# A sorting kernel: each row as two interleaved lanes of 512 places, merged by the last level

## The chip, the core and the metric

The kernel runs on one core of a Trainium2 chip. The core has five engines that run their own instruction streams and meet at semaphores: PE (TensorE, matrix products into the PSUM banks), DVE (VectorE, elementwise work on 128 partitions), ACT (ScalarE, activations), POOL (GpSimd, here only for gathers by index) and SP (SyncE, here only for transfers). The metric is the device time of one execution in microseconds (us). Smaller is better.

## What is computed

Eight images of 32 x 32 places with 128 channels pass through a deformable convolution, a self-correlation with a sort, a windowed attention, a mixture of experts, a state space model and a second mixture of experts. The part that matters here is the second one. Each image has 1024 tokens. For every token the correlation with all 1024 tokens is sorted in descending order and 128 fixed ranks of it are kept:

```python
def _L1_conv_ref(x):
    x3 = x.reshape(b, m, c)                      # m = 1024 tokens, c = 128
    corr = jnp.einsum('bmc,bnc->bmn', x3, x3) / c
    x_sort = jnp.sort(corr, axis=-1)[..., ::-1]
    ranks = jnp.round(jnp.linspace(1.0, m - 1, NB_POOLS)).astype(jnp.int32)
    return x_sort[..., ranks]
...
x = x + _L0_conv_ref(_gn(x), ...)
x = x + _L1_conv_ref(_gn(x))
t = t + _L2_attn_ref(...); t = t + _L2_ffn_ref(...)
t = t + _L3_attn_ref(...); t = t + _L3_ffn_ref(...)
```

## The kernel before

**Units.** The sort works in units of half an image: 4 tiles of 128 tokens, so that a buffer of a unit (`corr`, `srt_a`, `srt_b`) holds 4 x 1024 values in each of 128 partitions. There are 16 units, two for each image (h = 0 and h = 1), and the whole sort is done by DVE (`dve_S`).

**Streams.** Besides the sort (letter S) there are three streams. F is the front of the next image: group norm, the deformable convolution with its 24 groups of gathers (POOL gathers, PE and ACT combine), the second group norm, and the correlation (`pe_corr`, `act_corr`). C is attention, first experts and state space model of a half image that is already sorted. M is the second mixture of experts. Each engine runs one instruction stream, in which a table of letters (`ORDER`, one string for each engine and stage) says from which stream the next step is taken (`weave`). Nothing is reordered at run time: an instruction that waits holds up all that stands behind it on its engine. The stages are fill (F of image 0), early (sort of image 0 beside F of image 1), full (a body for each of the images 1 to 6, five of them in a loop), late (image 7) and drain.

**The first exchange is made by the correlation.** `sd` holds sums and differences of pairs of token columns. PE forms products with the sums and with the differences, ACT takes the absolute value of the latter, and PE adds and subtracts it, so that ACT writes to `corr` the larger and the smaller of each pair (L695, 512 values at a time). Before the change a pair is two columns 128 apart, and each write goes to runs of 128.

**The start of a unit.** `corr` is seen as 8 blocks of 128 places. The rest of a sorting network for 8 inputs runs across these blocks (L808 to L834 and again L808/L810), so that each of its operations reads and writes runs of 128. Its outputs have to become sorted groups of 8 neighbours, so the last results go to the view `Y`, with a step of 8 values (32 bytes) from one value to the next:

```python
X, L, R, Y = places(corr), places(srt_a), places(srt_b), corr[:].rearrange("p g (r s) -> p g s r", s=8)
```

`corr` is also used for this, so it is only given back to ACT (`corr_used`) once the first merge operation of runs of 16 (L796) has read it.

**The merges.** For run lengths m = 16 to 512 sorted runs are merged: a comparison of the two halves (`compare`, L794 the larger, L796 the smaller), then steps of distance k = m/4 down to 1 (L873 and L881 in one direction, L893 for the step m/8 in place, L901 and L903 back), with small copies of the edges (L877, L880) in the steps that change the buffer. Then the whole row of 1024 is merged by a comparison with the second half read backward (`hi[:, :, ::-1]`) and halvings down to 16, and only the places of the wanted ranks go through the last three steps (L927). L936 adds the ranks to the image; from there the stream C of this half starts.

**Links.** Dependent operations of one stream on DVE are tied by a semaphore (`link.put`, `link.wait`). `dve_gn` (L537, L540) takes the statistics of a group norm for F. L1073 on DVE needs the square root that ACT writes at L1063.

Of the kernel before, what the change touches and what calls it, by code (L numbers as in the profile page):

```python
# [62 lines left out]
        "FFFFFFFFFFFFFFCFFFFCCFFCFFCCCFFFFFCCFFFCCFCCFCCFFCCFFFFFFFFFFFFCCCCCCCCCCCCCCCCCCCCCCCCCCCCCCCCC"  # L63
# [3 lines left out]
        "FFFFFFFFFFFFFFFFFFFFFFFFFFFFFFFFFFFFFFFFFFFFFFFFFFFFCFCCFCFFFCCCFCCCFFFCCFFFFFFFFFFFFCCCCCCCCCCC"  # L67
# [42 lines left out]
    DVE_late=(  # L110
        "MCSSCMSSSSSSSSSSCCMSSCCMSSMSSSMSSCMSSCMSSSSSCSSCMCSSCMCSSCMSSSSSMSSSSMSSSSMSSSSSSSMSSCMSSCMSSSSM"
        "SSSSSCSSCSSCMSSCMCSSCCMSSCMSSCMCSSSSSCMSSMSSCCMSSSSCCMSSMSSCCMSSCMSSCMSSCMMSSMSSSSMSSMSMSMSMSMCS"
        "SCSSMSSSSMSSCCMSSCCMSSMSSCSSSCMSSSSCMCSSCMCSSSCMCSSSSMSSSSMSSSSSMSSSSSSCMSSCMSSSMSSSSSSCSSCMSSCM"
        "SSCMCSSSCCSSCMSSCMCMSSCSSMSSCCMSSMSSCSSSCSSCCSSSSCSSCSSCSSSSSSSSSSSSSSSSSSSS"
    ),
    DVE_drain=(
        "MCMCMMMMMMCCCMCMCMCMMCCCCCCMMMCMCCCMCMCCCCMCMCCMCMCCMMCCMCCMCCMCMMMMMMMMMMMMMMMMMMMMMMMMMMMMMMMM"
# [3 lines left out]
        "MCMCCCMMMMCMMCCCCCMMMMMMMCCMMMMMCCCCCMCCCMCCCMCCCCCCCCCCCMCCMMMCMMMCMCCCCCCCCMCMCMMMMMMMCMMCMMMC"  # L121
        "MMMMMCCMMMMMMCCMMMMCCMMMCMCMMMCMMMMMMMMMMMMMMMMMMMMMMMMMMMMMMMMMMMMMMMMMMMMMMMMMMMMMMMMMMMMMMMMM"
# [3 lines left out]
        "MCMCCMCMCCCMMCMCMMCMCCCMCMCMMCCMMCCCCCMCCCCCCCCCCCMMCMCCMCCCMCCCCCCCCCCCMMCMMCCMMMCMCMCMCMMCCMCM"  # L126
        "CCMCCMMCCMMMMMMMMMMMMMMMMMMMMMMMMMMMMMMMMMMMMMMMMMMMMMMMMMMM"
# [19 lines left out]
def build(nc, A, IMGS=IMAGES):  # L147
# [3 lines left out]
    with ctx:  # L151
# [65 lines left out]
        sd = sb("sd", [P, 2, 4, P])  # L217
# [395 lines left out]
        def pe_corr(pe, i, h):  # L613
# [4 lines left out]
            for t in range(4 * h, 4 * h + 4):  # L618
# [3 lines left out]
                sums, diffs = (sd[:, k].rearrange("p s r -> p (s r)") for k in range(2))  # L622
# [62 lines left out]
        def act_corr(act, i, h):  # L685
            for t in range(4 * h, 4 * h + 4):
# [1197 lines left out]
```

## Time and profile before

| | us |
|---|---|
| median of 3 executions | 4932.3 (4931.25 to 4941.95) |
| profiled execution | 4926.9 |
| its span | 4925.1 |
| DVE busy in the span | 4278.7 (87%) |
| PE busy in the span | 3975.1 (81%) |
| ACT busy in the span | 2954.3 (60%) |
| POOL busy in the span | 894.7 (18%) |

The span is the time from the first to the last instruction in the trace. Engines work beside each other, so busy times don't add up. Average shares hide the stages: DVE has nothing to sort before 248.65 us (fill) and after 4601 us (drain), and is busy nearly all of the time between. DVE starts its next instruction before the one before has quite ended: from start to start two independent operations lie some 0.08 us less apart than the duration of the first.

### The profile page before, as it was taken

How to read it: one execution, taken by the hardware profiler on the slowest of the kernel's cores; microseconds unless marked ns; L12 is line 12 of the kernel's file. 1: busy time of each engine (PE TensorE's matmuls, PEld its weight loads, DVE VectorE, ACT ScalarE, POOL GpSimd, SP SyncE). 2: the span in 40 equal slices, each digit the busy share in tenths (PEclk: the TensorE clock that was granted, in tenths of full speed). 3: DMA queues.
4: the chain of work that ended last, by engine and by line, in shares of the span. 5: the costliest groups of instructions: out<-in, count | busy, mean ns of one | idle time of the engine just before them, and what ended most of it. 6: DMA issues, size and time to landing. Idle time of an engine off the chain costs nothing.

```text
span 4925.1 us, 59870 instructions
## 1 busy us (share of the span) xinstructions
PE 3975.1 (81%) x19410; PEld 2674.8 (54%) x19410; DVE 4278.7 (87%) x5380; ACT 2954.3 (60%) x7241; POOL 894.7 (18%) x580
## 2 busy tenths in 40 slices
PE   5747748989798988989798988989798987767587
PEld 3616424667456654567456654566456653545354
DVE  1098999999999999999999999999999999999521
ACT  4526526687467846687467846687467855555452
POOL 2317000242005300242005300242005210000000
PEclk8878869999899988999799988999799988978798
DMA  4314100232013210232013210232013210010001
GB/s 131 98 35 124 35 0 18 75 101 69 5 43 110 79 36 18 75 102 68 7 43 110 79 36 18 67 104 67 13 43 109 71 40 13 22 29 27 10 22 39
DMA packets 226079, 269.71 MB, mean 55 GB/s; under 512 B 26831, under 2 KB 188506, under 8 KB 225626
## 3 DMA queue, kind: packets, MB, share of 16 engines
q0 software_dynamic: 46080, 151.03, 10.6%
q1 hardware_dynamic: 179674, 114.65, 7.9%
q8 instruction: 167, 2.74, 0.2%
q14 instruction: 158, 1.29, 0.1%
HBM read 242.25 MB, written 23.34 MB: 54 GB/s over the span
## 4 chain that ended last, share of the span: by engine, by line
PE 38%; DVE 33%; issue 12%; ACT 9%; DMA 4%; POOL 3%; SPq 1%; DVEq 0%; another core or an unknown queue 0%; ACTq 0%; POOLq 0%
PE bank L597 6%; PE bank L1633 4%; PE bank L1628 4%; PE bank L1613 3%; PE bank L1298 3%; POOL gath L759 3%; DMA gath<-quads,idx 3%; DVE srt_b L873 2%; DVE srt_b L881 2%; DVE srt_a L796 2%; DVE srt_b L796 2%; PE bank L569 2%; PE bank L1225 2%; PE bank L1218 2%; DVE srt_a L893 2%
## 5 line engine op out<-in xcount | busy, mean ns | idle before, releaser
L759 POOL DMA_INDIRECT gath<-quads,idx x576 | 894.5, 1553 | 3083.4 <-DVE idx L722 2005.3
L597 PE MATMUL bank<-diag,gath 128*128 128x128 f32 x4608 | 612.4, 295 | 167.6 <-DMA gath<-quads,idx 166.8
L639 ACT ACTIVATE diag<-ident,w 128x128 f32<-128x128 f32 x2304 | 704.6, 393 | 20.3 <-DVE w L737 20.2
L597 PEld LDWEIGHTS bank<-diag,gath 128*128 128x128 f32 x4608 | 591.3, 210 | 203.1 <-DMA gath<-quads,idx 126.9
L1613 PEld LDWEIGHTS bank<-e2w,act 128*128 128x128 f32 (+1 forms) x3072 | 409.8, 198 | 161.7 <-issue 157.3
L1628 PE MATMUL bank<-mu_t,e2w 128*128 128x512 f32 (+1 forms) x768 | 424.0, 635 | 86.4 <-DMA e2w<-moe_w_t 39.9
L1633 PE MATMUL bank<-gated_u,e2w 128*128 128x512 f32 (+1 forms) x768 | 426.1, 638 | 34.2 <-DVE act L1713 31.9
L1713 DVE TENSOR_TENSOR act<-act,bank 128x512 f32<-128x512 f32 (+1 forms) x384 | 261.3, 680 | 180.0 <-PE bank L1633 159.5
L1613 PE MATMUL bank<-e2w,act 128*128 128x128 f32 (+1 forms) x3072 | 415.0, 282 | 1.6 <-DVE act L1713 1.6
L873 DVE TENSOR_TENSOR srt_b<-srt_a 128x1024 f32<-128x1024 f32 x192 | 351.3, 1830 | 1.2
L881 DVE TENSOR_TENSOR srt_b<-srt_a 128x1024 f32<-128x1024 f32 x192 | 351.0, 1828 | 0.0
L1681 ACT ACTIVATE act<-bank 128x512 f32<-128x512 f32 (+1 forms) x384 | 227.7, 593 | 201.5 <-PE bank L1628 198.8
L1681 ACT ACT_TABLE_LOAD x199 | 255.3, 1283 | 11.9 <-PE bank L1628 8.8
L672 ACT ACTIVATE cols<-bank 128x384 f32<-128x384 f32 x192 | 93.0, 484 | 245.1 <-PE bank L597 235.7
L1633 PEld LDWEIGHTS bank<-gated_u,e2w 128*128 128x128 f32 (+1 forms) x768 | 131.3, 188 | 186.7 <-issue 140.0
L794 DVE TENSOR_TENSOR srt_b<-srt_a 128x2048 f32<-128x2048 f32 x96 | 219.6, 2287 | 1.4
L794 DVE TENSOR_TENSOR srt_a<-srt_b 128x2048 f32<-128x2048 f32 x96 | 219.5, 2286 | 0.9
L796 DVE TENSOR_TENSOR srt_a<-srt_b 128x2048 f32<-128x2048 f32 x96 | 219.2, 2284 | 0.0
L796 DVE TENSOR_TENSOR srt_b<-srt_a 128x2048 f32<-128x2048 f32 x96 | 219.2, 2283 | 0.0
L901 DVE TENSOR_TENSOR srt_a<-srt_b 128x2016 f32<-128x2016 f32 (+1 forms) x96 | 211.8, 2206 | 0.9
L903 DVE TENSOR_TENSOR srt_a<-srt_b 128x2016 f32<-128x2016 f32 (+1 forms) x96 | 211.7, 2205 | 0.0
L1628 PEld LDWEIGHTS bank<-mu_t,e2w 128*128 128x128 f32 (+1 forms) x768 | 122.1, 188 | 148.3 <-issue 62.1
(348 smaller groups left out, 8161.5 us busy)
## 6 DMA issues: line engine op xcount, KB each, us to landing
e2w<-moe_w_t SPq DMA_DIRECT2D x256, 170.5 KB
quads<-xn_tok SPq DMA_DIRECT2D x256, 64.0 KB
e1w<-L_ffn_w SPq DMA_DIRECT2D x256, 64.0 KB, 1.9
e2w<-moe_w_t SPq DMA_DIRECT2D x256, 64.0 KB
gath<-quads,idx POOLq DMA_INDIRECT x576
e2w<-moe_w_t SPq DMA_DIRECT2D x128, 42.5 KB
x_tok<-x SPq DMA_DIRECT2D x8, 512.0 KB, 4.1
out<-tm SPq DMA_DIRECT2D x16, 256.0 KB, 2.3
```

Of the source, the lines that this page charges most:

```text
L597: ins = T.matmul(FB[q % 2][:, k * P:(k + 1) * P], gath[:, g % 2, k, s * C:(s + 1) * C], diag[:, g % 2, 4 * k + s], start=(s == 0), stop=(s ...
L639: ins = SC.activation(diag[:, g % 2, n], ident[:], ACT.Copy, scale=w[:, n:n + 1])
L759: pool.indirect_dma_start(gath[:, g % 2, k], None, quads, bass.IndirectOffsetOnAxis(idx[:, TG * g + k:TG * g + k + 1], 0)).then_inc(sem["g ...
L794: V.tensor_tensor(dst[:, :, 0:size // 2], lo, hi, ALU.max)
L796: return V.tensor_tensor(dst[:, :, size // 2:size], lo, hi, ALU.min)
L873: V.tensor_tensor(out_lo, lo, hi, ALU.max)
L881: link.put(V.tensor_tensor(out_hi, lo, hi, ALU.min))
L1613: ins = T.matmul(MB[2][:, t * P:(t + 1) * P], act2[0:m, n % ACT2_SLOTS, t * P:(t + 1) * P], e2w[0:m, e % 2, W2 + k * C:W2 + (k + 1) * C], ...
L1628: T.matmul(MB[r % 2][0:m, :], e2w[:, e % 2, k * P:k * P + m], mu_t[:], start=True, stop=True).then_inc(sem["m_ps"], 1)
L1633: T.matmul(MB[r % 2][0:m, :], e2w[:, e % 2, W3 + k * P:W3 + k * P + m], gated_u[:], start=True, stop=True).then_inc(sem["m_ps"], 1)
L1681: SC.activation(act2[0:m, n % ACT2_SLOTS], MB[r % 2][0:m, :], ACT.Silu).then_inc(sem["m_sb"], 1)
L1713: V.tensor_tensor(act2[0:m, n % ACT2_SLOTS], act2[0:m, n % ACT2_SLOTS], MB[r % 2][0:m, :], ALU.mult).then_inc(sem["hh"], 1)
```

## The change

The row is held as two lanes of 512 places that are neighbours in memory: lane 0 at the even, lane 1 at the odd addresses. The pairs that the correlation exchanges are now the columns j and j + 512, and ACT writes the larger of two such columns and the smaller of them alternately, two values at a time at a step of 4. So each lane has sorted runs of two from the start. The network across 8 blocks is gone. The merges by halves start at m = 8 memory places (runs of four in each of two lanes) and go on to m = 1024, with steps down to k = 2, which is distance 1 within a lane. The runs of four have a short form of their own, with one operation in place and one copy. Then the two lanes are merged by one comparison, lane 0 forward against lane 1 backward, which also puts the lanes apart; the halvings go on from 512 as before. The strings of letters for the engines in the stages early, full, late and drain are new as well (two of the many lines are shown).

```diff
     PE_early=(
-        "FFFFFFFFFFFFFFFFFFFFFFFFFFFFFFFFFFFFFFFFFFFFFFFFFFFFFCFCCFCFFFCCCFCCCFFFCCFFFFFFFFFFFFCCCCCCCCCCC"
+        "FFFFFFFFFFFFFFFFFFFFFFFFFFFFFFFFFFFFFFFFFFFFFFFFFFFFFFFFFFFFCCCFCCCCCCCFFFFCCFFFFFFFFCCCCCCCCCCC"
...
-        sd = sb("sd", [P, 2, 4, P])
+        sd = sb("sd", [P, 2, HALF])
...
-                there = corr[:, t % UT].rearrange("p (s k r) -> p s k r", k=2, r=P)
+                there = corr[:, t % UT].rearrange("p (b k w) -> p b k w", k=2, w=2)
...
-                    SC.activation(there[:, :, k], FB[1 - k][:].rearrange("p (s r) -> p s r", r=P), ACT.Identity,
+                    SC.activation(there[:, :, k], FB[1 - k][:].rearrange("p (b w) -> p b w", w=2), ACT.Identity,
                                   scale=0.5 / C).then_inc(sem["corr_sb"], 1)
...
-            V.tensor_tensor(sd[:, 1], pairs[:, :, 0], pairs[:, :, 1], ALU.subtract)
-            V.tensor_tensor(sd[:, 0], pairs[:, :, 0], pairs[:, :, 1], ALU.add).then_inc(sem["sd"], 1)
+            V.tensor_tensor(sd[:, 1], yn_t[:, 0:HALF], yn_t[:, HALF:TOK], ALU.subtract)
+            V.tensor_tensor(sd[:, 0], yn_t[:, 0:HALF], yn_t[:, HALF:TOK], ALU.add).then_inc(sem["sd"], 1)
...
-            X, L, R, Y = places(corr), places(srt_a), places(srt_b), corr[:].rearrange("p g (r s) -> p g s r", s=8)
...
-            yield from exchange(fours(X, 0), fours(X, 1), fours(R, 0), fours(R, 1))
...
-            V.tensor_tensor(Y[:, :, 0], R[:, :, 0], R[:, :, 4], ALU.max)
-            link.put(V.tensor_tensor(Y[:, :, 7], R[:, :, 3], R[:, :, 7], ALU.min))
...
-            yield from exchange(L[:, :, 2:4], L[:, :, 4:6], R[:, :, 2:4], R[:, :, 4:6])
-            yield from exchange(R[:, :, 1:7:2], R[:, :, 2:7:2], Y[:, :, 1:7:2], Y[:, :, 2:7:2])
-            now = 1
-            m = 16
-            while m < TOK:
...
+            ins = yield from compare(8, runs(corr, 8), runs(srt_a, 8))
+            ins.then_inc(sem["corr_used"], 1)
+            yield
+            dve.wait_ge(sem["corr_used"], unit("corr_used", i, h))
+            now = 0
+            m = 8
+            while m <= TOK:
...
                 k = m // 4
-                while k >= 1:
+                while k >= 2:
                     lo, hi = pairs(here, k)
                     out_lo, out_hi = pairs(there, k)
                     link.wait()
                     V.tensor_tensor(out_lo, lo, hi, ALU.max)
                     yield
-                    if k == 1:
-
-                        V.tensor_copy(edges(there, 0, 1), edges(here, 0, 1))
+                    if m == 8:
+
+                        link.put(V.tensor_tensor(hi, lo, hi, ALU.min))
+                        yield
+                        link.wait()
+                        link.put(V.tensor_copy(lo, out_lo))
+                        yield
+                        break
+                    if k == 2:
+
+                        V.tensor_copy(edges(there, 0, 2), edges(here, 0, 2))
...
-            k = TOK
+            pair = bufs[now][:].rearrange("p g (j w) -> p g j w", w=2)
+            lo, hi = pair[:, :, :, 0], pair[:, :, ::-1, 1]
+            half = bufs[1 - now][:].rearrange("p g (w j) -> p g w j", w=2)
+            link.wait()
+            V.tensor_tensor(half[:, :, 0], lo, hi, ALU.max)
+            yield
+            link.put(V.tensor_tensor(half[:, :, 1], lo, hi, ALU.min))
+            yield
+            now = 1 - now
+            k = TOK // 2
```

What this makes of DVE's stream in one unit: 158 instructions become 157. 146 comparisons of two operands become 144, and the values that they write come to 184,304 in each partition, before and after. 12 copies (2,160 values) become 13 (3,184).

**Place 1: DVE, the first unit.** A row gives line, operation, output and inputs, and the shape of the output with its dimensions. Before, the end of the network across blocks and the first merge operations; the first and the third pair of rows write to `Y`:

```order
L833 TENSOR_TENSOR corr<-srt_b 128x512
L834 TENSOR_TENSOR corr<-srt_b 128x512
L808 TENSOR_TENSOR srt_b<-srt_a 128x4x256
L810 TENSOR_TENSOR srt_b<-srt_a 128x4x256
L808 TENSOR_TENSOR corr<-srt_b 128x4x3x128
L810 TENSOR_TENSOR corr<-srt_b 128x4x3x128
L794 TENSOR_TENSOR srt_a<-corr 128x256x8
L796 TENSOR_TENSOR srt_a<-corr 128x256x8
```

After, the unit's first rows, where nothing stands ahead of them:

```order
L791 TENSOR_TENSOR srt_a<-corr 128x512x4
L793 TENSOR_TENSOR srt_a<-corr 128x512x4
L830 TENSOR_TENSOR srt_b<-srt_a 128x512x2
L834 TENSOR_TENSOR srt_a<-srt_a 128x512x2
L837 COPY srt_a<-srt_b 128x512x2
L791 TENSOR_TENSOR srt_b<-srt_a 128x256x8
L793 TENSOR_TENSOR srt_b<-srt_a 128x256x8
L830 TENSOR_TENSOR srt_a<-srt_b 128x256x4
```

The rows of 128x512 and 128x4x3x128 into `corr` are gone, and the last reader of `corr` (L793) is the unit's second instruction, where it was its eighteenth (L796).

**Place 2: DVE, the end of the merges in the same unit.** Before, the last step of m = 512, the comparison of the whole row (L794 and L796 of 128x4x512, their second input read backward), the next halving:

```order
L901 TENSOR_TENSOR srt_a<-srt_b 128x8x255
L903 TENSOR_TENSOR srt_a<-srt_b 128x8x255
L794 TENSOR_TENSOR srt_b<-srt_a 128x4x512
L796 TENSOR_TENSOR srt_b<-srt_a 128x4x512
L794 TENSOR_TENSOR srt_a<-srt_b 128x8x256
L796 TENSOR_TENSOR srt_a<-srt_b 128x8x256
```

After, the last step of m = 1024, the comparison of the lanes (L877, L879), the next halving:

```order
L866 TENSOR_TENSOR srt_a<-srt_b 128x4x255x2
L868 TENSOR_TENSOR srt_a<-srt_b 128x4x255x2
L877 TENSOR_TENSOR srt_b<-srt_a 128x4x512
L879 TENSOR_TENSOR srt_b<-srt_a 128x4x512
L791 TENSOR_TENSOR srt_a<-srt_b 128x8x256
L793 TENSOR_TENSOR srt_a<-srt_b 128x8x256
```

The comparison of the whole row is replaced by one of the same size that reads every second value.

**Place 3: the stage early, behind the first unit.** DVE before; `lnsd` at L1073 is written by ACT (the square root of C's first norm):

```order
L936 TENSOR_TENSOR tc<-x2_tok,srt_a 128x512
L959 BN_STATS lnst<-tc 128x6 x4
L967 BN_AGGR lnmv<-lnst 128x2 x4
L808 TENSOR_TENSOR srt_b<-corr 128x8x256
L810 TENSOR_TENSOR srt_b<-corr 128x8x256
L1073 RECIPROCAL lnsd<-lnsd 128x4
L1074 SCALAR_TENSOR_TENSOR nmr<-lnmv,lnsd 128x4
L818 TENSOR_TENSOR corr<-srt_b 128x8x128
L820 TENSOR_TENSOR corr<-srt_b 128x8x128
```

DVE after, where L1047 is the former L1073:

```order
L910 TENSOR_TENSOR tc<-x2_tok,srt_a 128x512
L933 BN_STATS lnst<-tc 128x6 x4
L941 BN_AGGR lnmv<-lnst 128x2 x4
L791 TENSOR_TENSOR srt_a<-corr 128x512x4
L793 TENSOR_TENSOR srt_a<-corr 128x512x4
L1047 RECIPROCAL lnsd<-lnsd 128x4
L1048 SCALAR_TENSOR_TENSOR nmr<-lnmv,lnsd 128x4
L537 BN_STATS bst<-yn_t 128x6
L540 BN_STATS bst<-yn_t 128x6
L542 BN_AGGR mv<-bst 128x2
```

ACT before, where L672 and L639 are F's groups of gathers (a copy out of PSUM and twelve diagonal matrices for the group after next):

```order
L672 ACTIVATE cols<-bank0 128x384
L639 ACTIVATE diag<-ident,w4 128x128 x12
L1063 ACT_TABLE_LOAD
L1063 ACTIVATE lnsd<-lnmv,eps_ln 128x4
L672 ACTIVATE cols<-bank1 128x384
L639 ACTIVATE diag<-ident,w4 128x128 x12
L973 ACTIVATE tbu<-tc,nmr,lnsd 128x128 x4
L1079 ACTIVATE arena<-ident 128x4x96
L672 ACTIVATE cols<-bank0 128x384
```

ACT after, where L1037 is the former L1063:

```order
L672 ACTIVATE cols<-bank0 128x384
L639 ACTIVATE diag<-ident,w4 128x128 x12
L672 ACTIVATE cols<-bank1 128x384
L672 ACTIVATE cols<-bank0 128x384
L1037 ACT_TABLE_LOAD
L1037 ACTIVATE lnsd<-lnmv,eps_ln 128x4
L681 ACTIVATE xn_tok<-bank1 128x128
L521 ACTIVATE yn_t<-bank0 128x512
L521 ACTIVATE yn_t<-bank1 128x512
L947 ACTIVATE tbu<-tc,nmr,lnsd 128x128 x4
```

On ACT the square root stood behind 19 of image 1's 24 groups and now stands behind all 24; on DVE the statistics L537 and L540 of F now stand right behind its reciprocal, and stood behind 31 more rows, most of them of the sort.

## Rows read from the trace of the kernel before

**Rows 1.** The page's first part: busy us, share of the span, instructions.

```profile
PE 3975.1 (81%) x19410; PEld 2674.8 (54%) x19410; DVE 4278.7 (87%) x5380; ACT 2954.3 (60%) x7241; POOL 894.7 (18%) x580
```

**Rows 2.** Busy time by stretch: early, one full body, late, drain (header gives columns).

```profile
core 0: us, PE busy (x) PEld busy (x) DVE busy (x) ACT busy (x) POOL busy (x), PEclk, DMA share, GB/s
248.65:735.61 486.96, 283.25 (x1305) 195.65 (x1306) 466.09 (x477) 197.70 (x551) 113.28 (x72) 0.77 0.17 49
1842.10:2398.15 556.05, 484.76 (x2426) 328.10 (x2426) 533.41 (x672) 369.65 (x908) 118.92 (x72) 0.92 0.20 59
4067.29:4601.01 533.72, 366.49 (x1554) 228.53 (x1554) 520.56 (x624) 260.37 (x556) 0.00 (x0) 0.83 0.07 21
4601.01:4925.10 324.09, 262.08 (x1126) 167.21 (x1126) 77.91 (x214) 162.23 (x346) 0.00 (x0) 0.87 0.09 27
```

**Rows 3.** Groups of DVE instructions by shape: operation, count, busy us, mean ns, idle.

```profile
L794 DVE TENSOR_TENSOR srt_a<-srt_b 128x2048 f32<-128x2048 f32 x96 | 219.5, 2286 | 0.9
...
L808 DVE TENSOR_TENSOR corr<-srt_b 128x1536 f32<-128x1536 f32 x16 | 47.0, 2938 | 0.1
...
L833 DVE TENSOR_TENSOR corr<-srt_b 128x512 f32<-128x512 f32 x16 | 17.4, 1090 | 0.0
...
L927 DVE TENSOR_TENSOR srt_a<-srt_b 128x84 f32<-128x84 f32 x64 | 16.8, 304 | 0.0
...
L822 DVE TENSOR_TENSOR srt_a<-srt_b 128x512 f32<-128x512 f32 x16 | 10.9, 682 | 0.0
...
L877 DVE COPY srt_b<-srt_a 128x512 f32<-128x512 f32 x16 | 10.3, 642 | 0.0
...
L927 DVE TENSOR_TENSOR srt_b<-srt_a 128x336 f32<-128x336 f32 x16 | 8.0, 501 | 0.0
```

**Rows 4.** DVE in order of time, the unit's start: start us, us, operation.

```profile
1853.03 1.08 DVE L833 TENSOR_TENSOR corr<-srt_b 128x512 f32<-128x512 f32 x1
1853.95 1.10 DVE L834 TENSOR_TENSOR corr<-srt_b 128x512 f32<-128x512 f32 x1
...
1862.76 2.92 DVE L808 TENSOR_TENSOR corr<-srt_b 128x1536 f32<-128x1536 f32 x1
1865.53 2.92 DVE L810 TENSOR_TENSOR corr<-srt_b 128x1536 f32<-128x1536 f32 x1
```

**Rows 5.** DVE in order of time, in the merges (copies, dependent and independent neighbours).

```profile
1929.35 0.29 DVE L880 COPY srt_a<-srt_b 128x256 f32<-128x256 f32 x1
...
1931.60 2.16 DVE L901 TENSOR_TENSOR srt_b<-srt_a 128x1920 f32<-128x1920 f32 x1
1933.68 2.15 DVE L903 TENSOR_TENSOR srt_b<-srt_a 128x1920 f32<-128x1920 f32 x1
1935.86 2.23 DVE L873 TENSOR_TENSOR srt_a<-srt_b 128x1984 f32<-128x1984 f32 x1
...
3020.29 0.41 DVE L880 COPY srt_b<-srt_a 128x256 f32<-128x256 f32 x1
```

**Rows 6.** L794's instructions by form: duration ns min/median/max, first and last start.

```profile
L794 DVE TENSOR_TENSOR srt_b<-srt_a x96: 2259/2291/2294, 305.4 to 4590.3; 128x2048 f32<-128x2048 f32 x96
```

**Rows 7.** ACT's group of writes to `corr`, by shape.

```profile
L695 ACT ACTIVATE corr<-bank 128x512 f32<-128x512 f32 x128 | 74.6, 595 | 130.8 <-PE bank L627 54.3 <-PE bank L630 50.7 <-DVE srt_a L796 25.7
```

**Rows 8.** ACT in order of time, stage early: start us, us, operation, idle before.

```profile
273.80 1.08 ACT L695 ACTIVATE corr<-bank 128x512 f32<-128x512 f32 x2 [23.37 <-DVE srt_a L796]
...
294.49 1.08 ACT L521 ACTIVATE yn_t<-bank 128x512 f32<-128x512 f32 x2 [0.81 <-PE bank L510]
...
362.20 0.49 ACT L672 ACTIVATE cols<-bank 128x384 f32<-128x384 f32 x1 [3.56 <-PE bank L597]
...
481.33 0.49 ACT L672 ACTIVATE cols<-bank 128x384 f32<-128x384 f32 x1 [3.64 <-PE bank L597]
...
486.64 0.30 ACT L1063 ACTIVATE lnsd<-lnmv,eps_ln 128x4 f32<-128x4 f32 x1
```

**Rows 9.** DVE in order of time, stage early, behind the first unit.

```profile
471.49 2.28 DVE L810 TENSOR_TENSOR srt_b<-corr 128x2048 f32<-128x2048 f32 x1
486.97 0.18 DVE L1073 RECIPROCAL lnsd<-lnsd 128x4 f32<-128x4 f32 x1 [13.20 <-ACT lnsd L1063]
```

More of the change, by code:

```diff
@@ L94 @@
-        "CMSSCMSSMSSSSSSSCSSCMSSCMSSCMCSSCCMSSCMSSSCMCSSSSCSSCCSSSSCCFFSSCCFSSSSCFSSCFSSCSSSSSSSSSS"
+        "MCSSCMSSSSSMSSMCCMSSSCCMSSMSSMCSSSCSSMSSCMCSSCMCFCFCMFSSSMSSMSSSSSSSSSSSSSCMSSCMFSSMSSSSSSSSSCCS"
+        "SCMSSCMCSSCCMSSSSSCSSCSSCMFSSFSSCMFFSSCCMFSSCCMSSMSSSCSSCMSSSSCMSSCMSSCMSSSSMSSMSSMMSSMSSSSMSSMS"
+        "MSMSMSMCSSCSSSSSMSSSSSCCMSSCCMSSSSSSSSSCMSSCSSSMSSMCSSCSSCSSCMCSSSCMSSMSSSSMSSSSMSSSSSMSSSSSSMSS"
+        "CMSSCMSSSSSSSSSCSSCMSSCMSSCMCSSCCFFCMFSSSCMCMFSSCFSSMSSCSSCMSSCMCSSSSCCSSCSSCSSCSSSSSSSSSS"
@@ L621, in pe_corr @@
                 mine = yn_t[:, t * P:(t + 1) * P]
-                sums, diffs = (sd[:, k].rearrange("p s r -> p (s r)") for k in range(2))
+                sums, diffs = sd[:, 0], sd[:, 1]
                 T.matmul(FB[0][:], mine, diffs, start=True, stop=True).then_inc(sem["corr_mm"], 1)
@@ L742, in dve_pre @@
             dve.wait_ge(sem["corr_sb"], img("corr_sb", i, 0))
-            pairs = yn_t[:].rearrange("p (s k r) -> p s k r", k=2, r=P)
-            V.tensor_tensor(sd[:, 1], pairs[:, :, 0], pairs[:, :, 1], ALU.subtract)
-            V.tensor_tensor(sd[:, 0], pairs[:, :, 0], pairs[:, :, 1], ALU.add).then_inc(sem["sd"], 1)
+            V.tensor_tensor(sd[:, 1], yn_t[:, 0:HALF], yn_t[:, HALF:TOK], ALU.subtract)
+            V.tensor_tensor(sd[:, 0], yn_t[:, 0:HALF], yn_t[:, HALF:TOK], ALU.add).then_inc(sem["sd"], 1)
             yield
@@ L814, in fours @@
-            def fours(buf, b):
-                return buf.rearrange("p g (a b c) r -> p g a b (c r)", a=2, b=2)[:, :, :, b]
-            yield from exchange(fours(X, 0), fours(X, 1), fours(R, 0), fours(R, 1))
-            V.tensor_tensor(X[:, :, 1::4], R[:, :, 1::4], R[:, :, 2::4], ALU.max)
-            yield
-            link.put(V.tensor_tensor(X[:, :, 2::4], R[:, :, 1::4], R[:, :, 2::4], ALU.min))
-            yield
-            V.tensor_tensor(L[:, :, 3], R[:, :, 3], R[:, :, 7], ALU.max)
-            link.wait()
@@ L834, in dve_S @@
-            link.put(V.tensor_tensor(Y[:, :, 7], R[:, :, 3], R[:, :, 7], ALU.min))
-            yield
-            link.wait()
-            yield from exchange(L[:, :, 2:4], L[:, :, 4:6], R[:, :, 2:4], R[:, :, 4:6])
-            yield from exchange(R[:, :, 1:7:2], R[:, :, 2:7:2], Y[:, :, 1:7:2], Y[:, :, 2:7:2])
-            now = 1
-            m = 16
-            while m < TOK:
-                first = m == 16
-                if not first:
+            ins = yield from compare(8, runs(corr, 8), runs(srt_a, 8))
@@ L844, in dve_S @@
+            ins.then_inc(sem["corr_used"], 1)
+            yield
+            dve.wait_ge(sem["corr_used"], unit("corr_used", i, h))
+            now = 0
+            m = 8
+            while m <= TOK:
+                if m > 8:
                     link.wait()
-                ins = yield from compare(m, runs(corr if first else bufs[now], m), runs(bufs[1 - now], m))
-                if first:
-                    ins.then_inc(sem["corr_used"], 1)
-                else:
+                    ins = yield from compare(m, runs(bufs[now], m), runs(bufs[1 - now], m))
@@ L849, in dve_S @@
                     link.put(ins)
-                yield
-                if first:
-                    dve.wait_ge(sem["corr_used"], unit("corr_used", i, h))
-                now = 1 - now
+                    yield
+                    now = 1 - now
                 here, there = runs(bufs[now], m), runs(bufs[1 - now], m)
@@ L906, in dve_S @@
                 m *= 2
-            k = TOK
+            pair = bufs[now][:].rearrange("p g (j w) -> p g j w", w=2)
[6 more added lines that the diff above has]
+            yield
+            now = 1 - now
+            k = TOK // 2
             while k >= 16:
```

85 lines of the change are left out of this document (31 added, 54 removed).

## The prediction

> **What bounds the kernel now.** I read the busy times first: DVE is busy 87% of the span, PE 81% [rows 1]. The stretches say more. In a full body, of which there are six, DVE is busy 533.4 of 556.05 us and idle 22.6; PE is busy 484.8 of them at a granted clock of 0.92, and ACT 369.7. In late DVE is busy 520.6 of 533.7, in early 466.1 of 487.0, and only in drain does it have little to do [rows 2]. So from the first unit of the sort to the last, 248.65 to 4601 us, the time is DVE's own work plus 23 us of gaps for each image. What leaves DVE's stream there shortens the time nearly one for one, unless PE, which has 71 us of air in a full body, can't follow. Fill and drain lie on chains in which nothing of the sort changes.
>
> **What a comparison costs.** 2048 values take 2286 ns (L794) and 512 values 682 ns (L822) [rows 3]. That is (2286 - 682) / (2048 - 512) = 1.044 ns a value and 147 ns for the instruction. Neighbours that don't depend on each other start 2.08 us apart at a duration of 2.16 [rows 5], so on the path an instruction costs its duration less 0.08. Where the next one depends on it the distance is 2.18, 0.10 more [rows 5].
>
> **The slow writes go.** By this rule 1536 values cost 1.75 us, but the two writes of 1536 into `Y` take 2.94; and 512 values cost 0.68, but L833 takes 1.09 [rows 3]. These four operations (L808, L810, L833, L834) are the ones that write single values 32 bytes apart. From start to start they show 2.77 and 0.92 us [rows 4], where 1.67 and 0.60 would be due. Gone with them are 2 x 1.10 + 2 x 0.32 = 2.84 us in a unit. The number of compared values stays at 184,304, so the rest of the network across blocks is not saved: it comes back as merges of runs of four and as the level m = 1024. Two instructions fewer give 2 x 0.07 = 0.14.
>
> **What the new patterns cost.** Three forms are new. Runs of two values at a step of 32 bytes (L830, L834 at m = 8): L927 with 336 values (42 cells of 8, two of each) reads and writes just this form in 501 ns, and 147 + 336 x 1.044 is 498, so there is no surcharge; L927 with 84 values, which it reads singly 32 bytes apart, needs 304 where 235 would be due [rows 3]. Every second value, forward and backward (L877, L879): before, the whole-row comparison reads its second input backward by single values, and L794's longest of 96 took 2294 ns, 3 above the median [rows 6]; steps of two forward are in the last steps k = 1 of each merge. The two together are in no row. Upper bound: L833's rate, (1090 - 147) / 512 = 1.84 ns a value or 3.92 us for 2048, 1.55 us more on the path for each of the two, 3.1 in a unit; lower bound 0. I take 0, because these addresses lie 8 bytes apart and not 32. A gain I exclude: no comparison in the trace beats 1.04 ns. ACT's writes of two values at a step of four: 595 ns now [rows 7]; bounded above by the same surcharge of 0.41 us, 0 below. The 128 writes would cost 52 us of ACT, spread over a span in which ACT has 186 us of air in each full body [rows 2]; only the eight before the first unit would lie on the path, 3.3 us. I take 0.
>
> So the trace tells single values at 32 bytes (slow) from pairs at 32 bytes (not slow) [rows 3]. The Trainium skill gives a reason (Advanced Engine Details and Errata, SBUF Cachelines): lines of 16 bytes, and at least two hits on a line are needed for full rate. By that rule all three new forms have two hits and cost nothing extra, as I take it, and L833's form has one.
>
> **Copies.** The unit gets a copy of 1024 values in runs of two (L837). A copy of 256 takes 0.29 us where the values come in runs and 0.41 where they stand alone [rows 5]; 512 single ones take 0.64 [rows 3]. So 1024 in runs cost 0.15 + 4 x 0.14 = 0.71 us, 0.63 on the path, and at the rate of single ones 1.05. I take 0.63, as they come in runs. The other copies turn from single values into pairs, and those of the first merge (512 single ones) drop out: in sum 0.45 less. Net +0.2.
>
> **Links.** At m = 8 the operation in place, the copy and the next comparison each wait for the one before; two bare links at 0.10 us are 0.2, and about half as many go elsewhere. +0.1.
>
> **Sum for a unit:** -2.84 - 0.14 + 0.2 + 0.1 = -2.7 us. With 12 units in the full bodies and 2 in late this is -38 us, if PE and ACT follow. Why they should: `corr` is free again after the unit's second instruction, no longer after its eighteenth, so that the second half's correlation and with it F can start some 20 us earlier (30 in the full body), and the new tables have moved F forward on all engines. There PE and ACT get air just where the first 100 us of a body held them up.
>
> **The stage early** has the same -5.4 us for its two units, but a wait that grows. Before, ACT found `corr` free at 273.8 us [rows 8] (23 us of waiting for L796). After, the second comparison ends 4.4 us behind 248.65, at 253.1: F starts 20.7 us earlier, and its first copy of gathered columns (L672), 362.2 before, comes near 337, as DVE's own steps of F have moved up as well. The groups of gathers go by their own pace: the first was at 362.20 and the nineteenth at 481.33 [rows 8], 6.62 us each. But the square root that DVE needs now stands behind all 24 of them. The last one falls at 337 + 23 x 6.62 = 489, the square root at 491. DVE comes to its reciprocal 2.7 us earlier by the unit's gain and about 1.5 later by a wait for image 1's first transposes, near 472.5, and waits 18.5 us, where it waited 13.2 [rows 9]. Then it waits about 3 us more for `yn_t`, since the statistics of F stand right behind. So it is back at its sort 7 us later than before, less 2.7 of the second unit: early ends 4 us later. Bounds: 0 if POOL gets faster while DVE stands still, +10 if the pace doesn't hold. Queued behind the waiting reciprocal are the whole second unit and the first steps of C; PE and ACT have F to do meanwhile.
>
> **Total:** -38 + 4 = -34 us. The profiled execution's 4926.9 would become 4893, and the median 4932.3, which lies 5.4 above it, 4898.
>
> **The rivals.**
> - *All of it arrives, and the gaps shrink as well* (4882, 22%). If early loses nothing the sum is -43, 4889; with F earlier, DVE's gaps of 22.6 us in a full body could fall by one or two, 4877. For it: `corr` is free 30 us sooner. Against: the gaps stand at waits for PE within M, which isn't touched.
> - *PE takes over part of it* (4915, 13%). PE has 71 us of air in a full body, but not evenly, and M's steps stand later in the new tables of the second half. If half of the gain in the full bodies (12 x 2.7 / 2 = 16) turns into gaps, the sum is -18.
> - *The comparison of the lanes is slow* (4947, 8%). One mechanism, at L877 and L879: reading backward at a step of two costs what writing single values 32 bytes apart costs. 16 x 3.1 = 49 us, -34 + 49 = +15, slower. It decides against the change from 34 / 32 = 1.06 us for each of the 32 operations, that is from a duration of some 3.4 us. Against: rows 6 and the distance of 8 bytes; for: no row has both at once. The Trainium skill's rule on lines of 16 bytes (the same page) speaks against it too.
> - *The square root's wait recurs.* If what happens in early also happened in each full body, at 7 us, the sum would be +8 (4940). The tables speak against it: there the square roots of C stand behind the same ten groups as before (3%).
> - *It doesn't do what it says:* if the new forms had their slow price as well, nothing would have been won; that is the third rival.
>
> **How the numbers follow.** The forecast, -34, has 54%; the others have 22, 13, 8 and 3. The likeliest gives 4898, with 4888 to 4908 for its own bounds in early and for the copy. The range reaches to the gaps that shrink and to PE that takes over, with some of either's spread: 4874 to 4926. It leaves out the slow lanes (8), the recurring wait (3) and a tail of some 4 on each side. A difference of 0.2%, 10 us, is about what a measurement of this kernel can tell from no change. Faster by more: all of the second case, 51 of the 54 and 9 of the 13, 82%. Within it: 2 of the 54, 3 of the 13, 1 of the 8 and the recurring wait, 9%. Slower by more: 7 for the lanes and what is left, 9%.
>
> **What would show it.** In the profile after: no comparison of 512 or 1536 values over 1.8 us; L830 and L834 of 1024 values at 1.22; L837 at 0.7 (1.1 if it runs at single rate); L877 and L879 at 2.29 (3.4 or more would make the forecast wrong); L695 at 0.60. From one unit's start to the same unit's start an image later 550 to 551 us, where it is 556; DVE busy some 527 in it and idle 20 to 25. In early a wait of DVE at L1047 of 15 to 20 us with ACT as its cause. DVE's gaps over 30 us in a full body, at L1687 behind PE (the former L1713), would say that PE took over.

## The result and the profile after

The changed kernel takes 4943.0 us (median of 20 runs) where the kernel before, on the same chip, takes 4931.0 (20 runs). The ratio is 1.0023, with an interval of 1.0013 to 1.0034: slower by 0.23%, 12 us. The forecast was 34 us faster.

The profiled execution spans 4940.1 us (before 4925.1). First the page's busy times, share of the span and instructions:

```profile
PE 3925.9 (79%) x19410; PEld 2653.0 (54%) x19410; DVE 4237.4 (86%) x5364; ACT 2952.5 (60%) x7238; POOL 955.2 (19%) x580
```

DVE does 41.3 us less than in [rows 1], almost to the microsecond what the forecast took out of it (16 x 2.7 = 43). The new forms on DVE (groups by shape: count, busy us, mean ns, idle) and ACT's writes to `corr`:

```profile
L877 DVE TENSOR_TENSOR srt_b<-srt_a 128x2048 f32<-128x2048 f32 x16 | 36.7, 2291 | 0.4
L879 DVE TENSOR_TENSOR srt_b<-srt_a 128x2048 f32<-128x2048 f32 x16 | 36.6, 2286 | 0.0
...
L834 DVE TENSOR_TENSOR srt_a<-srt_a 128x1024 f32<-128x1024 f32 x16 | 19.5, 1220 | 0.0
...
L837 DVE COPY srt_a<-srt_b 128x1024 f32<-128x1024 f32 x16 | 11.1, 695 | 0.5
```

```profile
L695 ACT ACTIVATE corr<-bank 128x512 f32<-128x512 f32 x128 | 81.6, 638 | 96.8 <-PE bank L627 40.3 <-PE bank L630 34.1 <-DVE srt_a L793 22.3
```

The comparison of the lanes, forward and backward at a step of two, costs what any comparison of 2048 values costs, and the pairs at a step of 32 bytes cost 1220 ns for 1024 values. So the work shrank as intended and the time was lost elsewhere. Busy time by stretch (early, two full bodies, late, drain; columns as in [rows 2]) says where:

```profile
250.31:745.10 494.79, 286.30 (x1304) 201.25 (x1304) 460.64 (x472) 196.75 (x548) 120.18 (x72) 0.77 0.17 48
1862.14:2415.11 552.97, 470.82 (x2426) 318.14 (x2426) 527.86 (x670) 369.25 (x906) 130.22 (x72) 0.94 0.21 60
2415.11:2973.38 558.27, 472.19 (x2426) 319.54 (x2426) 528.32 (x669) 369.26 (x906) 128.45 (x72) 0.94 0.21 59
4088.56:4615.67 527.11, 381.15 (x1554) 236.80 (x1552) 514.88 (x619) 255.90 (x551) 0.00 (x0) 0.84 0.07 21
4615.67:4940.10 324.43, 260.13 (x1126) 166.19 (x1126) 77.94 (x214) 162.18 (x346) 0.00 (x0) 0.88 0.09 27
```

Late gives 6.6 us, drain nothing; early loses 7.8 in this profile, and the sort starts 1.7 us later. In a full body DVE is busy 5.1 to 5.6 us less, yet the body isn't shorter: 745.10 to 4088.56 is 557.2 us for each of the six, where 735.61 to 4067.29 of before was 555.3. That is some 7 us a body of new gaps against a forecast of none (DVE's idle time over the six is 25.1 to 35.8 us, 29.3 on average). PE isn't busy all the time either: it is busy 472 us of 558 at a granted clock of 0.94, less time than in [rows 2].

The largest new gap in the body from 2415.11 on stands 165 us behind its start. DVE (start us, us, operation, idle before and what ended it):

```profile
2579.97 0.69 DVE L1687 TENSOR_TENSOR act<-act,bank 128x512 f32<-128x512 f32 x1 [5.42 <-ACT act L1655]
```

ACT stood there for PE, and PE for an expert's weights:

```profile
2577.96 1.28 ACT L1655 ACT_TABLE_LOAD   x1 [10.25 <-PE bank L1602]
```

```profile
2575.79 2.07 PE L1602 MATMUL bank<-mu_t,e2w 128*128 128x512 f32 x2 [7.50 <-DMA e2w<-moe_w_t]
```

The weights are late because SP issues them late. SP's DMA issues (start us, time of issue, count), after:

```profile
2547.82 22.48 SPq L502 DMA_DIRECT2D quads<-xn_tok  x32
2570.48 0.52 SPq L1539 DMA_DIRECT2D e2w<-moe_w_t  x1
```

and before, a body that began at 2398.15:

```profile
2538.41 0.33 SPq L1565 DMA_DIRECT2D e2w<-moe_w_t  x1
...
2541.00 22.57 SPq L502 DMA_DIRECT2D quads<-xn_tok  x32
```

The 32 writes to `quads` hold SP for 22.5 us, 0.70 us each. Before, the load went ahead of them, 140.3 us into the body; after, behind them, at 155.4. The writes themselves did move forward, from 142.9 to 132.7 us into the body, and thereby past the load. It is one letter's place in a table that the prediction never read, SP's for the full body (C: an expert's weights of stage C, M: an expert's weights of stage M, the first two F: one half each of the writes to `quads`):

```diff
     SP_full=(
-        "CCCMMMCCCCCCCCMMFFMMMMMMMMCMCCCMCMMMF"
+        "CCCMMCMCCCCCCCMFFMMMMMMMMMCCCCMCMMFMM"
```

Five M stand ahead of FF before, four after.

### The profile page after: what moved, and what is told of

It reads as the page before. It is cut to its first block, busy times and chain, and to the rows that moved or that the text cites. A ratio compares the mean times of both kernels' runs of the same rounds, so it can differ in the third digit from the quotient of the medians.

```text
span 4940.1 us, 59852 instructions
## 1 busy us (share of the span) xinstructions
PE 3925.9 (79%) x19410; PEld 2653.0 (54%) x19410; DVE 4237.4 (86%) x5364; ACT 2952.5 (60%) x7238; POOL 955.2 (19%) x580
## 4 chain that ended last, share of the span: by engine, by line
DVE 36%; PE 33%; issue 12%; ACT 9%; SPq 4%; DMA 3%; POOL 2%; DVEq 0%; ACTq 0%; POOLq 0%
PE bank L597 6%; PE bank L1587 4%; DVE srt_b L846 3%; DVE srt_a L793 3%; PE bank L1272 3%; PE bank L1607 3%; SPq L502 3%; PE bank L1602 3%; DVE srt_b L793 3%; DVE srt_b L830 2%; DMA gath<-quads,idx 2%; DVE srt_a L791 2%; POOL gath L758 2%; DVE srt_a L858 2%; DVE srt_b L858 2%
## 5 line engine op out<-in xcount | busy, mean ns | idle before, releaser
L758 POOL DMA_INDIRECT gath<-quads,idx x576 | 955.0, 1658 | 3007.6 <-DVE idx L722 2085.7
L597 PE MATMUL bank<-diag,gath 128*128 128x128 f32 x4608 | 638.3, 303 | 221.6 <-DMA gath<-quads,idx 168.7
L597 PEld LDWEIGHTS bank<-diag,gath 128*128 128x128 f32 x4608 | 616.2, 217 | 264.9 <-DMA gath<-quads,idx 135.4
L639 ACT ACTIVATE diag<-ident,w 128x128 f32<-128x128 f32 x2304 | 704.6, 394 | 29.6 <-DVE w L737 29.6
L1687 DVE TENSOR_TENSOR act<-act,bank 128x512 f32<-128x512 f32 (+1 forms) x384 | 261.8, 682 | 233.8 <-PE bank L1607 159.2
L830 DVE TENSOR_TENSOR srt_b<-srt_a 128x1024 f32<-128x1024 f32 (+3 forms) x208 | 370.8, 1783 | 1.5
L846 DVE TENSOR_TENSOR srt_b<-srt_a 128x1024 f32<-128x1024 f32 x192 | 350.9, 1828 | 0.0
L791 DVE TENSOR_TENSOR srt_a<-srt_b 128x2048 f32<-128x2048 f32 x112 | 256.2, 2288 | 1.2
L793 DVE TENSOR_TENSOR srt_a<-srt_b 128x2048 f32<-128x2048 f32 x112 | 256.0, 2285 | 0.0
L672 ACT ACTIVATE cols<-bank 128x384 f32<-128x384 f32 x192 | 93.5, 487 | 258.2 <-PE bank L597 257.8
L791 DVE TENSOR_TENSOR srt_b<-srt_a 128x2048 f32<-128x2048 f32 x96 | 219.7, 2289 | 2.6 <-issue 1.3
L793 DVE TENSOR_TENSOR srt_b<-srt_a 128x2048 f32<-128x2048 f32 x96 | 219.4, 2285 | 0.0
L866 DVE TENSOR_TENSOR srt_a<-srt_b 128x2016 f32<-128x2016 f32 (+1 forms) x96 | 211.8, 2206 | 0.6
L868 DVE TENSOR_TENSOR srt_a<-srt_b 128x2016 f32<-128x2016 f32 (+1 forms) x96 | 211.7, 2205 | 0.0
```

The source lines that it names most:

```text
L597: ins = T.matmul(FB[q % 2][:, k * P:(k + 1) * P], gath[:, g % 2, k, s * C:(s + 1) * C], diag[:, g % 2, 4 * k + s], start=(s == 0), stop=(s ...
L639: ins = SC.activation(diag[:, g % 2, n], ident[:], ACT.Copy, scale=w[:, n:n + 1])
L758: pool.indirect_dma_start(gath[:, g % 2, k], None, quads, bass.IndirectOffsetOnAxis(idx[:, TG * g + k:TG * g + k + 1], 0)).then_inc(sem["g ...
L791: V.tensor_tensor(dst[:, :, 0:size // 2], lo, hi, ALU.max)
L793: return V.tensor_tensor(dst[:, :, size // 2:size], lo, hi, ALU.min)
L830: V.tensor_tensor(out_lo, lo, hi, ALU.max)
```

## The experiments

**1. The sort alone, and the load alone.** The theory was that the sort gives what it should and the new orders lose it, at this load above all. Two runs take it from both sides. The first has the new sort, and the orders of PE, ACT and SP of before; DVE's letters C, M and F were put after the same share of the sort's work as before. In DVE's table for the full body, start:

```diff
-        "MCSSCMSSSSSMSSMCCMSSSCCMSSMSSMCSSSCSSMSSCMCSSCMCFCFCMFSSSMSSMSSSSSSSSSSSSSCMSSCMFSSMSSSSSSSSSCCS"
+        "MCMSSCSSMSSSSMSSCCMSSSCCMSSSMSSMSSCSSCMSSSMSSCMCSSCMCSSCMCSSMSSSSSSSMSSSSSSSSCMFFCMSSFSSSFSSSSCS"
```

> The new sort alone: the changed kernel's sort, corr layout and SP work, but every hand-written order is the one of before. The tables of PE, ACT and SP are those of before letter for letter; in DVE's tables the C, M and F letters stand after the same share of the unit's sort work as before. Theory A (the sort saves what it should, the new orders lose it): all full bodies keep before's gaps of 17 to 20 us on DVE and DVE's busy time falls 5.4 us in each, so bodies of about 550 us, early about 482, in sum 4890 to 4905 us, ratio about 0.993. Rival B (DVE is not what bounds a full body; any DVE time saved turns into waits for PE and ACT, whatever the order): full bodies stay at 555 to 557 us, only early and late gain, in sum 4920 to 4930. Rival C (the sort's own new shapes cost more than their time, by slowing the others): at or over 4931.

4941.0 us, ratio 1.0014 (1.0004 to 1.0025). By the total, rival B or C. The second changes one letter's place in the changed kernel:

```diff
-        "CCCMMCMCCCCCCCMFFMMMMMMMMMCCCCMCMMFMM"
+        "CCCMMCMCCCCCCCMFMFMMMMMMMMCCCCMCMMFMM"
```

> The changed kernel with one letter of SP's full table moved: the next expert's weight load is issued between the two halves of the quads' writes instead of behind both. Theory A (the 7.5 us for which PE waits there for e2w makes the 5.4 us hole in DVE, once in each of six full bodies): the load is issued 11 us earlier, PE's wait at the first matmul of that expert is gone, each full body is 4 to 5 us shorter, in sum 4943 - 27 = about 4915 us. Rival B (PE's lateness there is taken up again before the body's end, or another wait of DVE comes in its place): the hole at 165 us goes but the body stays within 1.5 us, in sum 4935 to 4943.

4904.4 us, ratio 0.9944 (0.9930 to 0.9958), 39 us less than the changed kernel, more than theory A gave. It was run again later, on another chip:

> The changed kernel with the weight load between the two halves of the quads' writes once more, for comparison on the same chip: 4900 to 4910 us.

4901.7 us, ratio 0.9956 (0.9940 to 0.9971). The changed kernel itself was not measured again beside these runs, so the gain is best read from the ratios: from 1.0023 down by 0.79% and 0.67%, 39 and 33 us. What PE waited for expert weights of stage M in the whole execution (us in total, times, longest us), in the kernel before:

```profile
PE bank L1628 <- DMA e2w<-moe_w_t: 39.9, 19, 3.8
```

in the changed kernel:

```profile
PE bank L1602 <- DMA e2w<-moe_w_t: 85.6, 25, 7.9
```

with the load between the halves:

```profile
PE bank L1602 <- DMA e2w<-moe_w_t: 39.5, 20, 3.4
```

and DVE's waits at the product behind it, in the changed kernel and with the load between the halves:

```profile
DVE act L1687 <- ACT act L1655: 74.0, 29, 5.8
```

```profile
DVE act L1687 <- ACT act L1655: 42.9, 25, 3.6
```

46 us of PE's waiting and 31 of DVE's are gone, and PE waits as long as before the change. DVE's work is unchanged (4237.1), and the time falls by 33 to 39 us. The place of this one load made the difference, since nothing else was edited. In the two profiles the six bodies are 24 and 36 us shorter together.

**2. The load ahead of both halves,** as it stood before the change:

```diff
-        "CCCMMCMCCCCCCCMFFMMMMMMMMMCCCCMCMMFMM"
+        "CCCMMCMCCCCCCCMMFFMMMMMMMMCCCCMCMMFMM"
```

> The changed kernel with the same load moved ahead of both halves of the quads' writes, as it stood before the change. The slot comes free about 4.4 us after SP reaches the load, so the quads' writes start about 6 us later than in the changed kernel. If the gathers that read the quads are on the path, this loses up to 6 us in a full body against the load between the halves, and the sum is 4930 to 4945; if they have slack, the same as with the load between the halves, about 4915 by theory A.

4908.4 us, ratio 0.9945 (0.9923 to 0.9967): the same as between the halves, as far as six executions tell (4885 to 4929). In the bodies compared the load is issued 137.7 us into the body here and 143.7 with the load between the halves, and the writes to `quads` begin at 140.3 and 133.2. So both have some 6 us of slack in these orders. At 155.4 the load is too late: PE was ready for it at 153.2 (2575.79 less the wait of 7.50), and its multiplication began 5.3 us after the load was issued.

**3. Why the first run gained nothing.** Its trace has another loss than the changed kernel's: PE waits only 33.1 us for expert weights of stage M. The busy times of DVE's groups by shape, each counted by itself, add up to 4474 us, in the changed kernel to 4476, but the page's busy time, which counts overlaps once, is 26 us higher:

```profile
PE 3983.2 (81%) x19410; PEld 2676.1 (54%) x19410; DVE 4263.8 (86%) x5364; ACT 2960.3 (60%) x7241; POOL 862.6 (17%) x580
```

Placed by share of work, 45 of 83 pieces of other work in the full table had come to stand between the two halves of a comparison (maximum, minimum), which don't depend on each other; in the tables of before and after nearly all stand where the next sort instruction waits for the last. So the next run took before's tables letter for letter, which fits, since both sorts have 114 steps a unit.

> The new sort alone once more, now with all the order tables of before letter for letter, DVE's among them (a unit's sort has 114 steps in both kernels, and from the 17th on the two step through the same pattern of waits). In the first attempt 45 of 83 places in DVE's full table where other work follows the sort stood between the two halves of a comparison, and not at a place where the next sort instruction waits for the one before it; with before's letters it is 6 of 83. Theory A1 (the first attempt lost its gain by that: the sum of DVE's durations was the changed kernel's, but its busy time was 26 us more, since fewer of the waits between dependent sort instructions were covered): DVE busy about 4240 us in all and 528 in a full body, bodies 550 to 552, in sum 4895 to 4910 us. Rival B (PE and ACT bound the body whatever DVE does): DVE's busy time falls by the same 26 us and its gaps grow by as much, bodies 556 to 558, in sum 4925 to 4940.

4906.7 us, ratio 0.9948 (0.9931 to 0.9965), DVE busy 4238.0. Theory A1 foretold the time; B is out. The ratio is that of the new orders with the load repaired (0.9944, 0.9956, 0.9945): the new orders, even repaired, bring nothing over the old ones that these runs can tell. A full body of this run:

```profile
1835.88:2388.64 552.76, 481.46 (x2428) 323.80 (x2426) 528.38 (x670) 370.32 (x908) 119.85 (x72) 0.93 0.20 60
```

To have the interleaving by itself, one more run moved 132 letters of that table by one sort instruction, and nothing else. Its start:

```diff
-        "MCMSSCSSMSSSSMSSCCMSSCCMSSMSSMSSSCSSCMSSMSSCMCSSSCMCSSCMCSSMSSSSSSSMSSSSSSSSCMFFCMSSFSSSFSSSSCSS"
+        "MCMSSCSMSSSSSMSSCCMSCCMSSMSSMSSSCSSCMSSMSSCMCSSSCMCSSCMCSSMSSSSSSSMSSSSSSSSCMFFCMSSFSSSFSSSSCSSC"
```

> The new sort with all orders of before, as in the run with verbatim tables, except that in DVE's full table every piece of other work that stood where the next sort instruction waits for the one before it (132 letters) is put one sort instruction earlier, between the two halves of a comparison: 77 of 83 places instead of 6. Nothing is added or taken away, and a piece moves by 0.3 to 2.3 us. Theory A1: DVE's durations sum to the same 4473 us, but its busy time rises in each full body by more than the 3.5 us of the first attempt (45 of 83 places): 5 to 7 us, 30 to 42 us over six bodies and about 4270 to 4280 in all, and the kernel takes 4935 to 4950 us. Rival (where other work stands between the sort's instructions costs nothing, and the first attempt lost its time to the places of single pieces): busy time within 5 us of 4238, sum 4900 to 4912.

4936.9 us, ratio 1.0018 (1.0007 to 1.0030): 0.70% more than with before's letters, 34 us, for the same instructions. The body:

```profile
1841.85:2401.30 559.45, 483.72 (x2428) 326.47 (x2426) 533.77 (x670) 370.75 (x908) 116.06 (x72) 0.93 0.20 59
```

DVE's busy time is 5.4 us higher, as A1 said, and 33.6 in the whole execution (4271.6), as much as the time. In the first run it was 25.8 higher, for a loss of 0.66% or 33 us; the rest of that loss, some 7 us, stands in gaps and was not followed up. One place in both, in order of time; first before's letters, other work (L1687) ahead of the sort instruction that waits (L791 reads what L866 and L868 wrote):

```profile
1902.73 2.15 DVE L866 TENSOR_TENSOR srt_a<-srt_b 128x1920 f32<-128x1920 f32 x1
1904.80 2.15 DVE L868 TENSOR_TENSOR srt_a<-srt_b 128x1920 f32<-128x1920 f32 x1
1906.87 0.68 DVE L1687 TENSOR_TENSOR act<-act,bank 85x512 f32<-85x512 f32 x1
1907.46 2.28 DVE L791 TENSOR_TENSOR srt_b<-srt_a 128x2048 f32<-128x2048 f32 x1
```

then one step earlier:

```profile
1909.85 2.16 DVE L866 TENSOR_TENSOR srt_a<-srt_b 128x1920 f32<-128x1920 f32 x1
1911.93 0.68 DVE L1687 TENSOR_TENSOR act<-act,bank 85x512 f32<-85x512 f32 x1
1912.53 2.15 DVE L868 TENSOR_TENSOR srt_a<-srt_b 128x1920 f32<-128x1920 f32 x1
1914.71 2.29 DVE L791 TENSOR_TENSOR srt_b<-srt_a 128x2048 f32<-128x2048 f32 x1
```

From L866 to L791 4.73 us against 4.86. L1687 takes 0.6 us either way; but behind L868 the dependent L791 starts 2.18 us later in the second, where independent neighbours are 2.07 apart. It is the 0.10 us of a bare link of [rows 5], which other work covers here only when it stands in the link.

**4. The load too late, in the other order.** The run with before's letters, with its load moved between the halves too:

```diff
-        "CCCMMMCCCCCCCCMMFFMMMMMMMMCMCCCMCMMMF"
+        "CCCMMMCCCCCCCCMFMFMMMMMMMMCMCCCMCMMMF"
```

> The same with the next expert's weight load between the two halves of the quads' writes, where the order of before has it ahead of both. In the changed kernel the two places came to the same median (4904 and 4908 us). If the quads' writes have slack, the same here within 5 us of the run beside it; if PE is kept waiting for the gathers of the first quads, a gain of up to 6 us in a full body; if the load then comes too late for PE, a loss of 2 to 5 us in each.

4988.8 us, ratio 1.0113 (1.0094 to 1.0131): 82 us more, 14 in each full body, nearly three times the most that the third case allowed for. The trace shows what was overlooked. SP's issues with before's letters (body from 1835.88):

```profile
1971.91 0.33 SPq L1539 DMA_DIRECT2D e2w<-moe_w_t  x1
...
1974.48 22.78 SPq L502 DMA_DIRECT2D quads<-xn_tok  x32
```

and with the load between the halves (body from 1861.96):

```profile
2001.24 10.28 SPq L502 DMA_DIRECT2D quads<-xn_tok  x16
2011.71 0.53 SPq L1539 DMA_DIRECT2D e2w<-moe_w_t  x1
```

The load moves from 136.0 to 149.8 us, by 13.7 and not by the 10.3 of a half, because it now also stands behind SP's wait for `xn_tok`: the writes begin 139.3 us into the body, and ACT's first half of `xn_tok` (L651) ends at 139.0. PE stands 10.5 us for it, and C's matmuls behind it on PE as well, so that another operation of DVE is late:

```profile
2017.41 2.07 PE L1602 MATMUL bank<-mu_t,e2w 128*128 128x512 f32 x2 [10.49 <-DMA e2w<-moe_w_t]
```

```profile
2021.78 0.19 DVE L1480 TENSOR_TENSOR dtx<-dtx,ecum 128x32 f32<-128x32 f32 x1 [11.08 <-ACT ecum L1395]
```

This gap stands in each of the six full bodies (10.8 to 11.4 us). So the place between the halves is 33 to 39 us better than the one behind both in the new orders, and as good there as the one ahead; in the old orders it is 82 us worse than the one ahead. The reader explains both: PE was ready for this load 145.0 us into the body here, and 153.2 in the changed kernel. With some 5.5 us from issue to multiplication, 143.7 is early enough for the second, and 149.8 is 10 us too late for the first. How 10.5 us of PE's waiting become 14 in a body was not followed up.

**5. The stage early.** The changed kernel with early's tables of PE and ACT of before, and DVE's letters put after the same share of the sort. In ACT's:

```diff
-        "FFFFFFFFFFFFFFFFFFFFFFFFFFFFFCFFFCCCCCCFCCFCCCCFCFFCFCFFCFFFFFFCCCCCCCCCCCCCCCCCCCCCCCCCCCCCCCCC"
+        "FFFFFFFFFFFFFFCFFFFCCFFCFFCCCFFFFFCCFFFCCFCCFCCFFCCFFFFFFFFFFFFCCCCCCCCCCCCCCCCCCCCCCCCCCCCCCCCC"
```

> The changed kernel with the early stage's orders of PE, ACT and DVE as before (DVE's letters after the same share of the sort), all other stages unchanged. Theory A (the later place of the square root behind all the correlation groups makes early longer): early falls from 494.8 to 481 to 484 us, the wait at the reciprocal to about 13 us, and the sum falls by 11 to 14 us to about 4930. Rival (the first full body gives it back, since its F work then starts later): under 4 us.

4944.8 us, ratio 1.0028 (1.0015 to 1.0042). Early is 488.0 us, 6.8 less than in the changed kernel's profile; the first full body is 556.1, 3.2 more. The sum doesn't fall: the rival's side. But the 6.8 us can't be put down to the tables. With the load between the halves, early's tables are the changed kernel's, and SP issues the same transfers in the same order up to early's end; yet early is:

```profile
248.20:735.92 487.72, 281.31 (x1304) 195.93 (x1304) 460.58 (x472) 196.85 (x548) 119.09 (x72) 0.77 0.17 49
```

In its repeated run early is 487.9 us, with the load ahead of both halves 494.7. So these tables give 494.7 and 494.8 in two profiles and 487.7 and 487.9 in two others, and what makes the difference is not shown. Then before's tables for early letter for letter, DVE's too, with the load between the halves:

> The same, with the early stage's tables of before letter for letter as well. The early order of before alone brought nothing (the early stage 6.8 us shorter, the first full body 3.2 us longer, the sum unchanged within 2 us). If the early stage's square root costs where the full bodies are not late themselves: 5 to 7 us less than the run beside it, 4895 to 4900. If the first full body gives it back as before: within 3 us of it.

4900.2 us, ratio 0.9943 (0.9922 to 0.9964), beside 4901.7 for the load alone: no difference. The runs show no cost of the new early tables.

## Why the prediction was wrong

**DVE's work: right.** Slow writes, two instructions fewer, copies and links were to take 2.7 us from a unit; DVE's busy time fell by 41.3 us in 16 units, 2.6 each. L877 and L879 at 2.29, L830 and L834 at 1.22 and L837 at 0.70 us are the durations that it named. The Trainium skill's rule on lines of 16 bytes (Advanced Engine Details and Errata, SBUF Cachelines) agrees with all of them: these forms hit a line twice. The rival of the slow lanes fell.

**"If PE and ACT follow": the step that failed.** The prediction gave -38 us to 14 units in the full bodies and late, 32 of them to the full bodies, on the ground that "the new tables have moved F forward on all engines". The six bodies took 12 us more instead (557.2 against 555.3 each). Moving F forward on SP moved it ahead of an M. The 32 writes held SP's queue for 22.5 us, 0.70 each, and the load behind them came 15 us later in the body. The prediction costed DVE's instructions one by one and didn't take up SP's letters. Late, which has no writes to `quads`, gave 6.6 us where 5.4 were due. With the load repaired the full bodies take 553.3 and 551.3 us on average in the two profiles with the load between the halves, against a forecast of 550 to 551, and the kernel gains 22 to 28 us by the ratios where 34 were forecast, inside the range. With before's letters in all orders the sort is worth 26 us (ratio 0.9948).

**The rival "PE takes over part of it" named the place and not the cause.** It gave up half of the gain because PE has no even air. The gap does stand at L1687, but PE was idle itself, and the loss was more than the whole gain. DVE's idle time in a full body, foretold at 20 to 25 us with 30 as the sign of this rival, came to 25.1 and 29.9 in the two bodies shown, and to 35.8 in one of the six.

**Early: the mechanism right, the size right in two profiles of four.** The first copy of gathered columns was foretold for 337 us and came at 337.64. The last was foretold for 489 by 23 groups of 6.62 us, the square root for 491. In the changed kernel's profile:

```profile
494.61 0.49 ACT L672 ACTIVATE cols<-bank 128x384 f32<-128x384 f32 x1 [7.18 <-PE bank L597]
...
496.41 0.30 ACT L1037 ACTIVATE lnsd<-lnmv,eps_ln 128x4 f32<-128x4 f32 x1
```

So DVE waited 23.8 us at L1047 where 18.5 were due, and the pace of the groups was 6.82 us. With the load ahead of both halves it was the same (23.9). In the two profiles with the load between the halves, under the same early tables, the last copy came at 485.45 and 486.85, the pace was 6.53 us and the wait 16.8 and 16.7. The bound given (+10, "if the pace doesn't hold") covers both.

**How much of the miss is explained.** From the forecast of -34 us to the result of +11 by the ratio are 45 us. The load's place is 33 to 39 of them. The other 6 to 12 us lie between the repaired kernel and the forecast, and stay open. A part may be the long bodies described in the last section: the forecast had no term for bodies of one execution that differ by 9 us.

## What to carry to other kernels

- A saving on the bounding engine is worth its time only if each queue that the same change reorders still delivers. Read the tables of all queues, the DMA queue's too, for what now stands behind a block of issues: their count times what one takes in the trace (0.70 us here), plus the wait at the block's head. A place in a queue is right only with regard to when its readers come.
- When work of two streams is interleaved by hand on one engine, put the second stream's pieces where the first has a link between dependent instructions, not between its independent halves. Here one step to the side cost 0.7% with the same instructions.
- To try a part of a change alone, keep the old order literally. An order rebuilt by share of work had a loss of its own, larger than the gain that was to be measured (33 us against 26).

## What was not expected of the hardware

ACT's writes to `corr` in pairs at a step of four values take 638 ns where they took 595 [rows 7]: 0.04 us each, far from the 0.41 taken as a bound.

The bodies of one execution differ with the same orders and the same work. With the load between the halves:

```profile
1282.05:1832.41 550.36, 473.30 (x2426) 319.12 (x2426) 527.94 (x670) 369.33 (x906) 130.68 (x72) 0.94 0.20 60
1832.41:2392.15 559.74, 479.51 (x2426) 328.23 (x2426) 528.25 (x670) 369.70 (x906) 130.51 (x72) 0.93 0.20 59
```

DVE's busy time is the same within 0.3 us, PE's is 6 us longer at a clock granted a little lower, and the body is 9.4 us longer. DVE waits 14.1 us at L1687 in the longer one and 5.4 in the other, PE waits 17.6 us for gathered columns and 9.3. In the repeated run of this kernel the bodies span 546.6 to 556.5. With the load ahead of both halves four of six take 559.8 to 560.0, in the slowest execution of that kernel; with before's letters none is over 553.2. Whether the clock makes the gaps or they the clock was not settled.
